# Weights of a two-layer attention decoder: splitting them in front of the pipeline, or as steps of its filling

## The chip, the cores and the metric

The kernel runs on one core of a Trainium2 chip. The metric is the device time of one execution in microseconds (us). Engines: TensorE (PE), VectorE (DVE), ScalarE (ACT), GpSimd (POOL); SyncE (SP) issues most DMAs.

## What is computed

64 batch elements, each with x (256 tokens x 256 channels) and a context (77 x 256), all float32, pass through two layers:

```
# layer 0, 16 heads of 64
x = x + softmax((rms(x)*norm_w @ wq) @ (ctx @ wk).T) @ (ctx @ wv) @ wo
# layer 1, 16 heads of 16; ln has a gain and a shift
x = x + causal_mha(ln1(x), ln1(x)) @ m_proj_w + m_proj_b
x = x + mha(ln2(x), ctx)           @ c_proj_w + c_proj_b
x = x + relu(ln3(x) @ f_w1 + f_b1) @ f_w2 + f_b2
```

## The kernel before

**Precision.** PE multiplies in an fp32r format. A float32 operand that needs more is held as a high half (`wh`, a rounding copy by ACT) and a low half (`wl`, value minus high half, by DVE), and a product is three matmuls (lines 1102 to 1104). For the weights this is done once, together with two foldings: the gain of the norm ahead of a product is multiplied into the weight, and the norm's shift times the weight is added to the bias.

**Three parts.** The main work is a list of steps in three orders, one for each engine, written out by hand: `HEAD` fills the pipeline (batches 0 and 1), `LOOP` is one turn and runs NB - 3 = 61 times, `TAIL` empties it. A word such as `qs0.0.1@1:6` is a step (scores of layer 0, tile 0, group 1), its batch and the PSUM bank it takes. PE, ACT and DVE each follow their own order. `full[s]` and `free[s]` are the semaphores of bank s: PE raises the first when a bank is filled, the reader raises the second. SP and POOL walk PE's order and do what hangs on some of its steps. The steps named below:

- `ctx`, `turn.0`: PE transposes the context and the normalised x; ACT copies the high half, DVE makes the low half. `rms`, `stat`, `norm`: statistics and normalisation.
- `q0`, `k0`, `v0`, `ck`, `cv`, `q1`, `k1`, `v1`: projections. `k0` and `ck` read weights that are not split (`wk0`, `wck`).
- `qs0`: scores of layer 0. DVE takes maxima (`/0`), ACT exponentials and sums (line 717), DVE divides (`/1`). `tr0` transposes them, `pv0` multiplies by `v0`, `wo` projects.
- `qsA`, `qsB`, `ln`, `mt`, `skA`, `skB`, `pv.1`: causal attention of layer 1.

The loop's order starts with `pv.1.1` (line 1299), so the first matmul of that line behind HEAD marks the loop's start.

**The setup.** All this begins when the weights are ready. Ahead of it runs a serial block, once for each of the twelve entries of `WEIGHTS` (line 509; f1 first, then f2, mq, mk, mv, cq, cv, mp, cp, wv0, wq0, wo0). f1, f2, wv0, wq0 and wo0 have 1 MB each, the others 256 KB. Entry i uses staging buffer i % 3. SP loads it (line 590) when DVE has released the buffer (`w_free`) and PE has drained (`w_bias`, line 1074). ACT makes the high half (lines 814, 816), DVE the low half (line 847). PE multiplies the staged weight by the shift, in columns of one (line 1062; f1, mq, mk, mv, cq) or, for the three row biases (f2, mp, cp), by a bias spread over 128 columns (line 1071), and DVE adds the product (lines 855, 873). DVE also spreads biases (lines 861, 866) and makes small tables (lines 876, 879). wo0 and f2 share one pair of tiles, `tail_h` and `tail_l`; their halves are stored to DRAM (`store_parts`, lines 580 and 581) and loaded again by POOL in every turn. Behind the twelve weights SP issues the first x and context (lines 595, 596), `wk0` and `wck`. DVE then raises `consts_ready`, for which ACT and PE wait before their first step:

```python
            act.wait_ge(consts_ready, 1)
            nc.scalar.preload_act_table_set("natural_log_exp_and_others")
            orders(act, run)
```

## Time and profile before

| | before |
|---|---|
| three runs | 5188.43 us median (5183.74 to 5189.82) |
| the profiled execution | 5188.64 us |
| its span | 5186.8 us |
| busy in the span | PE 5008.5 us (97%), ACT 4150.4 (80%), DVE 3032.0 (58%), POOL 698.2 (13%) |
| mean granted clock of PE | 0.988 |

The profile shows one execution. Its span runs from the first to the last instruction; the execution's own time is 1.8 us longer. Times in the rows below count from the span's start. PEclk is TensorE's granted clock as a share of 2.4 GHz. "idle before" is the time that the engine stood still ahead of an instruction, and the arrow names what ended it.

### The profile page before, as it was taken

Reading aid. Unit: us, or ns where it says so; the run is one execution under the profiler, and the core shown is the slowest. Engines: PE = TensorE matmul, PEld = TensorE weight load, DVE = VectorE, ACT = ScalarE, POOL = GpSimd, SP = SyncE. Lnnn points to the kernel's source line nnn. Section 1 sums busy time; section 2 is a strip of 40 time slices with the busy share of each in tenths; the row PEclk is TensorE's granted clock in tenths of the full one; section 3 lists DMA queues with packets and bytes.
Section 4 is the critical chain, followed back from the end, with each engine's and each line's share of the span. In section 5 each row is a group of like instructions: output and inputs, shape, how many; then the busy total and the mean of one; then the engine's idle time right before and its main releaser. Section 6 shows DMA issues by size and latency. Waiting matters only on the chain.

```text
span 5186.8 us, 148622 instructions
## 1 busy us (share of the span) xinstructions
PE 5008.5 (97%) x49240; PEld 4129.3 (80%) x49240; DVE 3032.0 (58%) x7921; ACT 4150.4 (80%) x17044; POOL 698.2 (13%) x1227
## 2 busy tenths in 40 slices
PE   7999999999999999999999999999999999999997
PEld 5788888888888888788888888888888888888875
DVE  4556655655655665665556556556656655565553
ACT  5788888888888888888888888888887888888874
POOL 0111111111111111111111111111111111111110
PEclk7999999999999999999999999999999999999997
DMA  3212112112112112121121121121121221211211
GB/s 111 74 45 76 62 56 79 62 56 78 62 56 78 49 70 78 42 76 67 53 76 62 56 79 62 56 78 57 62 78 44 74 76 44 76 62 56 79 58 37
DMA packets 101414, 337.76 MB, mean 65 GB/s; under 512 B 8720, under 2 KB 66896, under 8 KB 68048
## 3 DMA queue, kind: packets, MB, share of 16 engines
q0 software_dynamic: 36576, 266.35, 14.0%
q1 hardware_dynamic: 64496, 68.39, 4.0%
q14 instruction: 316, 2.59, 0.2%
q8 instruction: 26, 0.43, 0.0%
HBM read 313.74 MB, written 20.97 MB: 65 GB/s over the span
## 4 chain that ended last, share of the span: by engine, by line
PE 51%; ACT 30%; issue 10%; DVE 8%; DVEq 0%; DMA 0%; ACTq 0%; PEldq 0%; POOL 0%; SPq 0%; PEld 0%; POOLq 0%
ACT ps L717 23%; PE ps L1102 7%; PE ps L1104 6%; PE ps L1103 6%; PE ps L1282 5%; PE ps L1190 4%; PE ps L1299 4%; PE ps L1271 3%; DVE negmax L930 3%; PE ps L1260 3%; PE ps L1233 2%; PE ps L1248 2%; PE ps L1266 2%; ACT k0bd L697 2%; PE ps L1214 2%
## 5 line engine op out<-in xcount | busy, mean ns | idle before, releaser
L717 ACT ACTIVATE ps<-ps,negmax 128x77 f32<-128x77 f32 (+2 forms) x6144 | 2058.1, 366 | 308.2 <-DVE negmax L930 306.5
L717 ACT ACTIVATION_READ_ACCUMULATOR ps<-ps,negmax 128x1 f32 x6144 | 1455.7, 243 | 0.7
L930 DVE TENSOR_REDUCE negmax<-ps 128x4 f32<-128x308 f32 (+2 forms) x1792 | 923.6, 563 | 224.0 <-PE ps L1200 93.0
L651 POOL TENSOR_TENSOR small<-small 128x1 f32<-128x1 f32 (+1 forms) x448 | 257.9, 576 | 2556.8 <-DVE small L907 2300.7
L1102 PE MATMUL ps<-tail_h,coTh 128*128 128x256 f32 x2048 | 594.7, 290 | 3.9 <-DVE coTl L1030 3.4
L925 DVE TENSOR_TENSOR zTl<-ps,zTh 128x256 fp32r<-128x256 f32 x512 | 210.8, 422 | 628.0 <-ACT zTh L697 627.8
L1103 PE MATMUL ps<-tail_l,coTh 128*128 128x256 f32 x2048 | 574.2, 280 | 0.0
L1104 PE MATMUL ps<-tail_h,coTl 128*128 128x256 f32 x2048 | 572.9, 280 | 0.0
L789 ACT ACTIVATE probs<-ps 128x512 f32<-128x512 f32 x768 | 398.8, 616 | 130.3 <-PE ps L1271 130.3
L1102 PEld LDWEIGHTS ps<-tail_h,coTh 128*128 128x128 f32 x2048 | 386.5, 189 | 43.1 <-issue 34.6
L1103 PEld LDWEIGHTS ps<-tail_l,coTh 128*128 128x128 f32 x2048 | 387.4, 189 | 0.0
L1104 PEld LDWEIGHTS ps<-tail_h,coTl 128*128 128x128 f32 x2048 | 387.0, 189 | 0.0
L697 ACT COPY probs<-ps 77x512 f32<-77x512 f32 x512 | 285.7, 588 | 87.0 <-PE ps L1233 86.5
L1190 PE MATMUL ps<-k0bd,q0T 128*128 128x154 f32 x2048 | 351.1, 301 | 1.2 <-ACT ps L717 0.7
L697 ACT CAST zTh<-ps 128x256 fp32r<-128x256 f32 x512 | 192.9, 389 | 183.1 <-PE ps L1306 152.5
L1190 PEld LDWEIGHTS ps<-k0bd,q0T 128*128 128x128 f32 x2048 | 288.2, 191 | 31.3 <-issue 21.2
L786 ACT ACTIVATE probs<-ps 77x512 f32<-77x512 f32 x512 | 255.2, 602 | 70.4 <-PE ps L1248 70.4
L1102 PE MATMUL ps<-zTh,hi_f 128*128 128x256 f32 x1024 | 303.9, 297 | 5.8 <-issue 1.9
L1102 PE MATMUL ps<-xTh,hi_wq 128*128 128x256 f32 x1024 | 293.5, 287 | 0.3 <-ACT ps L717 0.3
L1103 PE MATMUL ps<-xTl,hi_wq 128*128 128x256 f32 x1024 | 286.4, 280 | 0.0
L1104 PE MATMUL ps<-xTh,lo_wq 128*128 128x256 f32 x1024 | 286.2, 279 | 0.0
L1103 PE MATMUL ps<-zTl,hi_f 128*128 128x256 f32 x1024 | 286.1, 279 | 0.0
(207 smaller groups left out, 12303.4 us busy)
## 6 DMA issues: line engine op xcount, KB each, us to landing
tail_h<-parted_f POOLq DMA_DIRECT2D x64, 1024.0 KB, 5.1
tail_l<-parted_f POOLq DMA_DIRECT2D x64, 1024.0 KB, 7.0
tail_h<-parted_wo POOLq DMA_DIRECT2D x63, 1024.0 KB, 5.2
tail_l<-parted_wo POOLq DMA_DIRECT2D x63, 1024.0 KB, 7.1
xin<-x_dram SPq DMA_DIRECT2D x64, 256.0 KB, 3.4
x<-x_dram SPq DMA_DIRECT2D x64, 256.0 KB, 2.7
out<-xr SPq DMA_DIRECT2D x64, 256.0 KB, 2.2
cin<-ctx_dram SPq DMA_DIRECT2D x64, 77.0 KB
```

The lines of the kernel that those rows point to most:

```text
L651: nc.gpsimd.tensor_tensor(rstd[:, stage, ts], veps[:, stage, ts], minus_half[:, ts], ALU.pow).then_inc(rstd_ready[stage], 1)
L697: return nc.scalar.copy(o, i)
L717: ins = nc.scalar.activation(scores, scores, ACT.Exp, bias=negmax[w][:, t, h:h + 1], accum_out=sums[w][:, t, h:h + 1])
L786: nc.scalar.activation(probs_slot(step, r)[0:S], bank(s)[0:S, :], ACT.Exp).then_inc(free[s], 1)
L789: nc.scalar.activation(probs_slot(step, r), bank(s), ACT.Exp).then_inc(free[s], 1)
L925: nc.vector.tensor_tensor(lo, src, hi, ALU.subtract).then_inc(free[s], 1)
L930: nc.vector.tensor_reduce(dst, bank(s)[:, 0:heads * width].rearrange("p (h k) -> p h k", h=heads), AX_X, ALU.max, negate=True).then_inc(ma ...
L1102: pe.matmul(o, lh, rh, start=first, stop=False)
L1103: pe.matmul(o, lh, rl, start=False, stop=False)
L1104: return pe.matmul(o, ll, rh, start=False, stop=last)
L1190: ins = pe.matmul(bank(s)[:, j * 2 * S:(j + 1) * 2 * S], q0T[:, m, t * P:(t + 1) * P], k0bd[:, m, :, :], start=True, stop=True)
L1282: ins = pe.matmul(bank(s)[D0 * e:D0 * e + D0, j * T:(j + 1) * T], v0[0:S, D0 * h:D0 * h + D0], probs_slot(("tr0", 0, i), e)[0:S, j * T:(j ...
```

## The change

The serial block is gone. What it did becomes three kinds of steps in HEAD's orders: `w.i` (split weight i: ACT's high half, DVE's low half), `b.i` (the product of weight i with a shift or a spread bias on PE, added by DVE; it takes a PSUM bank as any step) and `g.0` (the small tables, on DVE). `WEIGHTS` has a new order, and each entry its own staging place, in tiles that HEAD does not use yet (f1 and f2 in `probs1`, wv0 in `probs0`, wq0 in `q0T`, mq and mk in `k1bd`, cv in `z1`, mp in `x1`, ...); only wo0, cq and cp are loaded into a place that another had before. The gains, shifts and biases go from `probs0` to `logs`. PE waits for a weight (`have`) at the step of batch 0 that reads it. SP issues the first x and context, the small tables, and nine weights without a wait. The rest of HEAD's three orders and its banks are new too; LOOP and TAIL are as they were.

```diff
 HEAD_ORDER_TEXT = """
+ctx@0:0 rms@0 turn.0@0:1 k0.0@0:2 k0.1@0:3 q0.2@0:4 q0.1@0:5 q0.3@0:6 qs0.0.1@0:7 qs0.1.1@0:0 q0.0@0:1 rms@1
+v0.0@0:2 b.2@0:4 b.6@0:3 qs0.0.0@0:5 qs0.1.0@0:6 tr0.1.1@0:1 tr0.0.1@0:0 qs0.0.3@0:2 b.3@0:7 tr0.1.0@0:4 b.4@0:1
+b.5@0:0 b.8@0:6 tr0.0.0@0:7 qs0.0.2@0:3 b.9@0:5 qs0.1.2@0:4 pv0.1@0:2 tr0.0.3@0:3 qs0.1.3@0:4 pv0.0@0:7
+tr0.1.2@0:3 tr0.0.2@0:6 v0.1@0:6 tr0.1.3@0:3 pv0.2@0:4 pv0.3@0:6 ck@0:1 cv@0:0 ctx@1:5 b.10@0:3 wo.0@0:6
+stat.1.0@0 wo.1@0:4 k0.1@1:1 k0.0@1:2 stat.1.1@0 norm.1.0@0 norm.1.1@0 turn.1.1@0:0 turn.1.0@0:7 turn.0@1:5
+k1@0:3 q1.1@0:6 q0.1@1:4 qsB.0@0:1072 qsA@0:5364 q0.0@1:1 v1@0:0 qs0.0.1@1:7 q0.3@1:6 qs0.1.1@1:5 q0.2@1:2
...
 HEAD_ACT_ORDER_TEXT = """
+ctx@0 w.0@0 turn.0@0 k0.0@0 w.1@0 q0.2@0 k0.1@0 q0.1@0 w.2@0 q0.3@0 w.3@0 q0.0@0 qs0.1.1@0 qs0.0.1@0 v0.0@0 w.4@0
+w.5@0 w.6@0 w.8@0 w.7@0 tr0.1.1@0 qs0.1.0@0 tr0.0.1@0 qs0.0.0@0 qs0.0.3@0 tr0.1.0@0 w.11@0 w.9@0 qs0.0.2@0
+qs0.1.2@0 w.10@0 tr0.0.0@0 pv0.1@0 tr0.0.3@0 qs0.1.3@0 tr0.0.2@0 tr0.1.2@0 pv0.0@0 v0.1@0 tr0.1.3@0 pv0.2@0
+pv0.3@0 ck@0 ctx@1 cv@0 k0.1@1 turn.1.1@0 turn.1.0@0 k0.0@1 turn.0@1 k1@0 q1.1@0 q0.1@1 qsB.0@0/0 qsB.0@0/1
...
 HEAD_DVE_ORDER_TEXT = """
+rms@0 ctx@0 norm.0@0 w.0@0 turn.0@0 w.1@0 rms@1 w.2@0 qs0.0.1@0/0 qs0.1.1@0/0 w.3@0 qs0.1.1@0/1 qs0.0.1@0/1 b.2@0
+qs0.1.0@0/0 qs0.0.0@0/0 qs0.0.3@0/0 w.8@0 qs0.1.0@0/1 b.3@0 b.6@0 qs0.0.0@0/1 qs0.0.3@0/1 w.4@0 w.5@0 qs0.0.2@0/0
+w.7@0 qs0.1.2@0/0 w.9@0 qs0.0.2@0/1 qs0.1.2@0/1 w.10@0 qs0.1.3@0/0 b.8@0 w.11@0 qs0.1.3@0/1 w.6@0 b.4@0 b.5@0
+b.9@0 g.0@0 pv0.3@0 pv0.2@0 pv0.1@0 pv0.0@0 norm.0@1 ctx@1 b.10@0 wo.0@0 stat.1.0@0 norm.1.0@0 wo.1@0 stat.1.1@0
...
+        WEIGHTS = [("wq0", 0, None, flat(q0T)), ("wv0", None, None, flat(probs0)), ("f1", 3, 2, half[0]),
+                   ("f2", None, None, half[1]), ("mq", 1, 0, pair[0]), ("mk", 1, 0, pair[1]), ("mv", 1, 0, flat(q1T)),
+                   ("cv", None, None, flat(z1)), ("mp", None, None, flat(x1)), ("cq", 2, 1, half[1][:, 0:512]),
+                   ("cp", None, None, half[1][:, 512:1024]), ("wo0", None, None, half[0])]
...
@@ SP
+            sp.dma_start(xin[:], x_v[0]).then_inc(x_in, 16)
+            sp.dma_start(cin[0:S, :], ctx[0]).then_inc(c_in, 16)
+            for tile, n in small:
+                sp.dma_start(tile, w[n]).then_inc(consts_in, 16)
+            sp.dma_start(bias_h[:], w["f1b"]).then_inc(consts_in, 16)
+            for i in range(NUMBER["cq"]):
+                load(i)
+                if i < 2:
+                    tile, n = ((wk0, "wk0"), (wck, "ck"))[i]
+                    sp.dma_start(tile[:], w[n].rearrange("(k p) n -> p k n", p=P)).then_inc(plain_in[i], 16)
+            sp.dma_start(row[:, :, :], w["rows"].unsqueeze(0).to_broadcast([P, 3, C])).then_inc(rows_in, 16)
+
+            sp.wait_ge(x_used, 1)
+            sp.dma_start(xin[:], x_v[1]).then_inc(x_in, 16)
+            sp.wait_ge(c_used, 1)
+            sp.dma_start(cin[0:S, :], ctx[1]).then_inc(c_in, 16)
+
+            sp.wait_ge(w_lo, LO_COUNT[NUMBER["f1"]])
+            sp.wait_ge(hidden_spread, 1)
+            load(NUMBER["wo0"])
+            store_parts("f2")
+            sp.wait_ge(rows_made, ROW_COUNT["f2"])
+            load(NUMBER["cq"])
+            load(NUMBER["cp"])
+            sp.wait_ge(w_lo, LO_COUNT[NUMBER["mp"]])
+            sp.wait_ge(rows_made, ROW_COUNT["mp"])
             sp.dma_start(x1[:], x_v[0]).then_inc(xres_in, 16)
             store_parts("wo0")
@@ POOL
-                        if isinstance(b, int):
-                            pool.wait_ge(parts_out, 64)
...
+                if part.settle:
+
+                    pool.wait_ge(parts_out, 64)
@@ ACT
+                    elif n == "w":
+
+                        i = step[1]
+                        name, g, _, _ = WEIGHTS[i]
+                        act.wait_ge(w_in[i], 16)
+                        if name == "wo0":
+                            act.wait_ge(parts_out, 32)
...
+                        if isinstance(b, int) and b == 0:
+                            act.wait_ge(tables_made, 1)
...
-            act.wait_ge(consts_ready, 1)
+            act.wait_ge(consts_made, 9)
             nc.scalar.preload_act_table_set("natural_log_exp_and_others")
@@ DVE
+            def split_low(i):
+
+                n, g, _, _ = WEIGHTS[i]
                 src = staged(i)
+                dve.wait_ge(w_hi, HI_COUNT[i])
...
+            def add_product(u, i):
+
+                n, _, shifted, _ = WEIGHTS[i]
+                (s, v, _), = u["bank"]
+                dve.wait_ge(full[s], v)
...
+                if n == "f1":
+                    for k in range(MF):
+                        done(nc.vector.tensor_copy(hidden_rows(k), bias_h[:, k:k + 1].to_broadcast([P, P])))
+                    done(nc.vector.tensor_scalar(minus_bias[:], bias_h[:], -1.0, None, ALU.mult))
+                    dve.sem_inc(hidden_spread, 1)
@@ PE
-            for _ in range(30):
-                pe.wait_ge(consts_in, 16 * 4)
-            pe.wait_ge(consts_ready, 1)
-            pe.wait_ge(plain_in, 32)
+            for _ in range(26):
+                pe.wait_ge(consts_made, 9)
...
+            NEEDED = {"q0": "wq0", "v0": "wv0", "cv": "cv", "wo": "wo0", "tr0": "wv0"}
+
+            def have(n):
+
+                pe.wait_ge(w_lo, len(WEIGHTS) if n == "wo0" else LO_COUNT[NUMBER[n]])
+
+            def bias_product(u, i):
+                s = take_bank(u)
+                n, _, shifted, _ = WEIGHTS[i]
+                src = staged(i)
+                pe.wait_ge(w_in[i], 16)
...
+                    pe.wait_ge(hidden_spread if n == "f2" else value_spread, 1)
...
+                    if isinstance(b, int) and b == 0 and n in NEEDED:
+                        have(NEEDED[n])
+                    if n == "b":
+                        bias_product(u, step[1])
```

## Rows read from the trace of the kernel before

**Rows 1.** Windows: from:to, length, busy PE, PEld, DVE, ACT, POOL, PEclk, DMA, GB/s

```profile
0.00:55.40 55.40, 23.23 (x88) 19.74 (x88) 25.56 (x54) 17.91 (x20) 3.51 (x13) 0.74 0.66 229
...
64.51:92.28 27.77, 26.09 (x194) 22.36 (x194) 14.28 (x39) 22.42 (x92) 0.70 (x1) 0.95 0.01 2
92.28:147.01 54.73, 45.27 (x364) 33.72 (x364) 19.46 (x49) 34.44 (x138) 3.43 (x6) 0.81 0.02 7
...
147.01:225.67 78.66, 77.31 (x768) 64.29 (x768) 45.25 (x116) 64.57 (x266) 10.04 (x17) 1.00 0.18 63
...
304.53:4955.63 4651.10, 4563.56 (x45322) 3769.47 (x45321) 2772.01 (x7258) 3808.49 (x15695) 641.31 (x1122) 1.00 0.18 65
4955.63:5186.80 231.17, 187.61 (x1705) 147.99 (x1704) 106.52 (x276) 136.32 (x564) 27.64 (x48) 0.87 0.15 53
```

**Rows 2.** Waits in the setup: who waited for whom: us, times, longest

```profile
SPq L589 <- PEq L1074: 30.4, 9, 10.3
...
ACT hi_mv L816 <- DMA probs<-mv_dram: 7.9, 1, 7.9
```

**Rows 3.** Timeline of SP's DMA issues: start us, us, instruction

```profile
0.75 0.39 SPq L583 DMA_DIRECT2D bias_h<-f1b_dram  x1
...
2.62 0.95 SPq L590 DMA_DIRECT2D probs<-f_dram  x2
...
41.98 0.58 SPq L595 DMA_DIRECT2D xin<-x_dram  x1
```

**Rows 4.** Timeline of PE's matmuls: start us, us, instruction, idle before it

```profile
21.43 2.51 PE L1071 MATMUL ps<-probs,xr 128*128 128x256 f32 x8
...
24.21 1.02 PE L1062 MATMUL ps<-probs,q0T 128*128 128x1 f32 x8 [0.27 <-issue]
...
56.90 3.69 PE L1173 MATMUL ps<-cT,wk 128*128 128x77 f32 x16 [0.96 <-DVE cTl L925]
...
90.47 2.01 PE L1173 MATMUL ps<-cT,wk 128*128 128x77 f32 x16
```

**Rows 5.** Timeline of the setup: start us, us, instruction, idle before it

```profile
8.05 1.28 ACT L816 ACT_TABLE_LOAD   x1 [8.05 <-DMA probs<-f_dram]
...
8.12 6.96 PE L1062 MATMUL ps<-probs 128*128 128x1 f32 x32 [8.12 <-DMA probs<-f_dram]
9.35 2.19 ACT L816 ACTIVATE hi_f<-probs 128x1024 fp32r<-128x1024 f32 x2
...
11.64 2.48 DVE L847 SCALAR_TENSOR_TENSOR lo_f<-probs,hi_f 128x1024 fp32r<-128x1024 f32 x2 [6.08 <-ACT hi_f L816]
...
15.42 1.01 DVE L866 COPY xs<-bias_h 128x128 f32<-128x128 f32 x4
...
17.85 2.29 DVE L847 SCALAR_TENSOR_TENSOR tail_l<-probs,tail_h 128x2048 fp32r<-128x2048 f32 x1 [0.16 <-DVE minus_bias L867]
```

**Rows 6.** Windows, columns as in rows 1

```profile
5.00:10.00 5.00, 1.88 (x9) 1.91 (x10) 0.52 (x2) 1.93 (x2) 0.00 (x0) 1.00 1.05 384
...
66.00:67.00 1.00, 1.00 (x6) 1.00 (x6) 0.41 (x4) 0.00 (x0) 0.44 (x1) 0.50 0.00 0
```

**Rows 7.** Groups by line on DVE, 64.44 to 92.48 us: busy us, mean ns

```profile
L930 DVE TENSOR_REDUCE negmax<-ps 128x4 f32<-128x308 f32 x8 | 3.8, 476 | 5.5 <-PE ps L1190 5.3
L925 DVE TENSOR_TENSOR coTl<-ps,coTh 128x512 fp32r<-128x512 f32 x4 | 2.7, 686 | 3.9 <-ACT coTh L697 3.9
...
L972 DVE RECIPROCAL over<-sums 128x4 f32<-128x4 f32 x8 | 1.4, 176 | 2.7 <-ACT ps L717 2.5
```

**Rows 8.** Windows, columns as in rows 1

```profile
118.50:135.70 17.20, 14.29 (x90) 8.91 (x93) 7.54 (x20) 13.53 (x67) 0.00 (x0) 0.51 0.00 1
```

**Rows 9.** Chain that ended last, at the loop's entry: start us, us

```profile
145.96 1.05 issue
```

**Rows 10.** Timeline of PE at the first turn's jump

```profile
225.47 0.28 PE L1104 MATMUL ps<-tail_h,coTl 128*128 128x256 f32 x1
225.67 0.42 PE L1299 MATMUL ps<-probs,v 128*32 128x256 f32 x4
```

More of the change, by code:

```diff
@@ L100 @@
+b.9@0 g.0@0 pv0.3@0 pv0.2@0 pv0.1@0 pv0.0@0 norm.0@1 ctx@1 b.10@0 wo.0@0 stat.1.0@0 norm.1.0@0 wo.1@0 stat.1.1@0
+norm.1.1@0 turn.1.1@0 turn.1.0@0 turn.0@1 qsB.0@0/0 qsB.0@0/1 qsB.0@0/2 qsA@0/2 qsB.0@0/3 qsA@0/0 qsA@0/1 qsA@0/3
+qs0.0.1@1/0 qs0.1.1@1/0 qs0.0.1@1/1 qsB.1@0/0 qsB.1@0/2 qsB.1@0/3 qs0.0.0@1/0 qsB.1@0/1 qs0.0.3@1/0 qs0.1.0@1/0
+ln.1@0 qs0.1.0@1/1 qs0.1.1@1/1 qs0.0.0@1/1 qs0.0.3@1/1 pv.1.0@0
 """
@@ L604, in run @@
                     more = not isinstance(b, int) or b + 1 < NB
-                    if step == ("turn", 0) and more:
+                    first = isinstance(b, int) and b == 0
+                    if step == ("turn", 0) and more and not first:
                         sp.wait_ge(x_used, b + 1)
                         sp.dma_start(xin[:], x_at(x_v, b + 1)).then_inc(x_in, 16)
-                    elif n == "ctx" and more:
+                    elif n == "ctx" and more and not first:
                         sp.wait_ge(c_used, b + 1)
@@ L789, in run @@
                         nc.scalar.activation(probs_slot(step, r), bank(s), ACT.Exp).then_inc(free[s], 1)
+                    elif n == "w":
[5 more added lines that the diff above has]
+                        src = staged(i)
+                        for k in pieces(i):
+                            if g is None:
+                                ins = nc.scalar.copy(wh[name][:, k, :], src[:, k, :])
+                            else:
+                                ins = nc.scalar.activation(wh[name][:, k, :], src[:, k, :], ACT.Copy,
+                                                           scale=gain[:, g, k.start:k.stop])
+                        ins.then_inc(w_hi, 1)
                     elif n == "q1":
                         s = landed(u)
+                        if isinstance(b, int) and b == 0:
+                            act.wait_ge(tables_made, 1)
                         for m in range(KT):
@@ L806, in _ @@
             act.wait_ge(consts_in, 16 * 4)
-            for i, (n, g, s) in enumerate(WEIGHTS):
-                act.wait_ge(w_in[i % 3], 16 * (i // 3 + 1))
-                if n == "wo0":
-                    act.wait_ge(parts_out, 32)
-                src = staged(i)
-                for k in pieces(i):
-                    if g is None:
-                        nc.scalar.copy(wh[n][:, k, :], src[:, k, :]).then_inc(w_hi, 1)
-                    else:
-                        nc.scalar.activation(wh[n][:, k, :], src[:, k, :], ACT.Copy,
-                                             scale=gain[:, g, k.start:k.stop]).then_inc(w_hi, 1)
-            act.wait_ge(consts_ready, 1)
+            act.wait_ge(consts_made, 9)
             nc.scalar.preload_act_table_set("natural_log_exp_and_others")
@@ L1050, in _ @@
         def _(pe):
[L1051 to L1080 removed]
             for bank_full in full:
                 pe.sem_inc(bank_full, FIRST)
+            pe.wait_ge(consts_made, 9)
+            for _ in range(26):
+                pe.wait_ge(consts_made, 9)
             def take_bank(u, j=0):
@@ L1098, in landed @@
                         pe.wait_ge(free[s], v)
+            NEEDED = {"q0": "wq0", "v0": "wv0", "cv": "cv", "wo": "wo0", "tr0": "wv0"}
[4 more added lines that the diff above has]
+                n, _, shifted, _ = WEIGHTS[i]
+                src = staged(i)
+                pe.wait_ge(w_in[i], 16)
+                if shifted is not None:
+                    pe.wait_ge(consts_in, 16 * 4)
+                    for m in range(src.shape[2] // P):
+                        for k in range(KT):
+                            ins = pe.matmul(bank(s)[:, m:m + 1], src[:, k, m * P:(m + 1) * P], shift[:, shifted, k:k + 1],
+                                            start=(k == 0), stop=(k == KT - 1))
+                else:
+                    e = ("mp", "cp", "f2").index(n)
+                    pe.wait_ge(hidden_spread if n == "f2" else value_spread, 1)
+                    for k in range(src.shape[1]):
+                        rows = hidden_rows(k) if n == "f2" else z[:, e, k * P:(k + 1) * P]
+                        ins = pe.matmul(bank(s)[:, 0:C], rows, src[:, k, :], start=(k == 0), stop=(k == src.shape[1] - 1))
+                ins.then_inc(full[s], 1)
             def three(o, lh, ll, rh, rl, first, last):
@@ L1166, in run @@
                     elif n in ("k0", "ck"):
+                        if isinstance(b, int) and b == 0:
+                            pe.wait_ge(plain_in[0 if n == "k0" else 1], 16)
                         landed(c, u, step)
```

184 lines of the change are left out of this document (72 added, 112 removed).

## The prediction

> **What bounds the kernel now.** I read the windows first, cut at landmarks, because the change touches only what lies ahead of the loop. Four stretches of the span can be told apart [rows 1]. Up to 55.40 us the setup runs: TensorE (PE) is busy 23.2 us of it, VectorE (DVE) 25.6, ScalarE (ACT) 17.9, so three engines are each less than half full, one after another. Then comes the filling (HEAD) up to 147.01 us, when the first matmul of the loop's order starts. Then come 61 turns: (4955.63 - 147.01) / 61 = 78.83 us each, with PE busy 98% at a granted clock of 1.00. The last 231.17 us are the TAIL, which the diff leaves alone. The loop is 93% of the span and its text is not changed either. So the whole question is where the 147.01 us end, and whether a turn keeps its 78.83 us.
>
> Inside the setup the view of waits says why it is so loose [rows 2]: SP sat for 30.4 us in nine waits for PE's drain, because each of the three staging buffers is loaded again only when PE, ACT and DVE have left it; ACT then waits for the transfers behind it, once for 7.9 us. The first batch's x is issued only at 41.98 us, behind all weights [rows 3]. The reader is to see a chain load, split, drain, load, and no engine that is full.
>
> **The change, part by part.** I work out three stages: A, up to the first q0 product (before: 64.51 us); B, up to the first wo product (before: 92.28 us, 27.77 long); C, up to the loop (before: 147.01 us, 54.73 long) [rows 1, 4].
>
> *Stage A.* Twelve staging places replace three, so the loads are issued back to back: x, ctx, four small tables, then wq0 as the seventh. An issue costs SP 0.39 to 0.58 us [rows 3], so after six of them from 0.75 us on wq0 is issued at about 3.5 us. The first weight of the kernel before went out at 2.62 and PE could start on it at 8.12 [rows 3, 5]: 5.5 us. So wq0 lands at 9.0. It is cast on ACT (2.19 us, the row of f1, same size) up to 11.2 and subtracted on DVE (2.48 us) up to 13.7 [rows 5]. wk0 lies behind it on the same queue: 1.05 MB at 384 GB/s [rows 6] is 2.7 us, and with some slack for what shares the queue I set 11.9. The steps of ctx and of x's statistics need only x, ctx, GpSimd's identity and ACT's table load, all there by about 6 us, and are hidden behind wk0. PE then runs k0.0 and k0.1. Before, the first k0 matmul stood at 56.90, k0.0 took 3.69 us [rows 4], and q0 began at 64.51, 7.6 us later with x's turn in between; without it I take 7.4. The first q0 product starts at 11.9 + 7.4 = 19.3 instead of 64.51: 45.2 us earlier. Bounds: 17.5 (wk0 close behind wq0, no wait between) and 21.3 (both large transfers slowed as f1 and f2 were beside mq and the rows).
>
> Which clock do those products get? The granted clock reads 1.00 from the first microsecond, yet 32 matmuls of one column took 6.96 us at 8.12 (0.22 each) and eight of the same shape 1.02 us at 24.21 (0.13 each) [rows 4 to 6]. The durations decide: PE, idle up to 8 us, worked at its lower level of 1.2 GHz then and at 2.4 GHz later, and I take k0 at the lower one, as before at a granted clock of 0.50. The Trainium skill (TensorE: Matmul & The Clock Gate, Part 1: The HAM clock gate) says that the throttled clock is the default and that activity releases it; the durations agree with it and the column does not. By the column k0.0 and k0.1 would cost 2.01 us each, as the k0 at 90.47 does [rows 4], and stage A would end 3 us earlier.
>
> *Stage B* takes over most of what was setup. PE: its own busy time is 26.09 us; turn.0 and k0.0 of batch 1 leave for stage C (0.60 and 2.01), which leaves 23.5. The products come in. At the fast rate eight of the 128x1 matmuls take 1.02 us [rows 4]; f1 is 32 and mq, mk, mv, cq are 8 each, so eight such groups are 8.2. f2 is 16 of the 128x256 ones at 2.51 us per eight [rows 4], mp and cp are 4 each: 24 / 8 x 2.51 = 7.5. Sum 15.7, PE 39.2 us. At the rate of the setup it is 23.2 instead of 15.7 [rows 1]. DVE: 14.28 + 25.56, less 2.48 (w.0, stage A), 1.3 (x's statistics) and 0.69 (turn.0 of batch 1) = 35.4. ACT: 22.42 + 17.91, less 2.56 (two table loads), 2.19 (w.0) and 1.4 (k0.0 and turn.0 of batch 1) = 34.2. So three engines come out near 34 to 39 us: the stretch is no longer one engine's, and each wait between them shows.
>
> Walking the three orders with these durations: v0.0 ends on PE at 29; f1's product at 33; DVE has then done w.1, w.2, w.3, adds the product and makes eight spread copies (1.01 us for four, [rows 5]) by 36. Behind that one mark three things queue. PE's f2 product (b.3, 5.0 us) runs 37 to 42. SP issues wo0 and the two stores of f2's halves, 3.1 MB: at 384 GB/s 8.2 us plus some 2 us to land, so 46; ACT meets w.11, which waits for these stores, at 43 and stands for 3 us, and behind w.11 wait w.9, qs0.0.2 and all that follows on ACT. cq and cp are issued behind f2's product at 43 and land at 47, so b.9 waits there too. DVE after 36 still has six maxima (0.48), six divisions (a reciprocal of 0.18 and a multiply over the same 308 columns, taken as 0.48), eight low halves (2.29 for the 1 MB one, the others by their size, 7.9 in all), the other product adds with mv's four spreads (2.5), the small tables (2.4) and four context splits (0.69): 22.3 us of work and, by this walk, 5 us of waits, up to 63.3 [rows 5, 7]. wo.0 needs the last of them. Stage B is 63.3 - 19.3 = 44.0 us. Bounds: 39.2, PE's sum with no wait; and 52, PE at the slow rate (46.7) and 5 us of waits on top.
>
> *Stage C* has nothing of the setup but keeps its own work, and gets k0.0 and turn.0 of batch 1, 2.6 us. k0 goes into the hole between wo.1 and the turns, where q0.1 was, which moves behind q1.1. I add 1.6 us, between nothing and 2.6: 56.3. Of this stage 17.20 us ran at a granted clock of 0.51, beginning after a stretch where ACT's exponentials held PE up [rows 1, 8]. The new order has the same softmax blocks there, so I keep it. If it stayed at 1.00 up to 5 us would go, if the slow stretch grew by as much 4 would come: 50 to 60.
>
> What else is moved costs nothing on this path. The cp product (b.10), 4 matmuls in front of wo.0, is counted above. The x1 load comes behind the mp product near 47 and lands 16 us before DVE reads it. ACT's q1, k1 and ck wait for the small tables (61), as ck does by the walk for about 1 us, but only stage C reads kcbd. GpSimd's wait for the stores moves from wo.1 to the end of HEAD; they land long before, and no loop instruction gains a wait.
>
> **Sum.** The loop starts at 19.3 + 44.0 + 56.3 = 119.6 us instead of 147.01: 27.4 us earlier. The profiled execution took 5188.64 us (span 5186.8, 1.8 around it), the median of the runs is 5188.43, so I take the difference from the median: 5161.0.
>
> **Rivals.**
> 1. *The setup vanishes wholly.* Stages at their lower bounds: 17.5 + 39.2 + 50 = 106.7, that is 5148. For it: PE's idle time in B and C together is 11 us [rows 1]. Against: ACT is full for long in B and the chain through w.11. Chance 0.12.
> 2. *The engines take turns.* At the upper bounds 21.3 + 52 + 60 = 133.3, that is 5175; with PE slow in all of B and C's slow stretch too, some 5180, about no change. For it: the slow clock as late as 67 us, and again in C [rows 6, 8]. Against: PE has work without a break from 12 us on. Chance 0.10 beyond my range, a third of it within 0.2% of no change.
> 3. *A turn gets longer (the other side).* All engines' code ahead of the loop changes length, and a turn starts with a jump back. The price is that of one stall on the path a turn: at the entry to the loop the chain has 1.05 us of issue [rows 9]. 61 x 1.05 = 64 us, less 27: 5225. It decides from 27.4 / 61 = 0.45 us a turn (0.6 to be slower by over 0.2%). Against: at the jump of the first turn PE goes from its last matmul at 225.47 to the next at 225.67, with no stall to be seen [rows 10]; and the first turn, which was entered without a jump, is no shorter than the rest by more than 0.2 us [rows 1]. The Trainium skill (Runtime: NRT & Kernel Launch, Instruction fetch mechanics) says that a jump to code that is not held forces a fetch and a stall; by that rule where the loop begins in the code matters, and before, PE shows no such stall. Chance 0.06.
> 4. *It does not do what it says:* a step placed early on ACT or DVE waits for a late transfer and holds up all behind it, as if the setup were still serial. w.11 would have to be late by 17 more us to bring the gain to 10. Chance 0.04.
>
> **How the numbers follow.** My forecast has 0.68, with 5151 to 5172 as its own range. Rivals 1 and 2 lie at 5148 and 5175 to 5180. A range of 5149 to 5174 leaves out about a fifth: the outer halves of 1 and 2, and 3 and 4. Within 0.2% is within 10.4 us, about what a measurement of this kernel can tell from no change. Faster by more: all of the forecast and rival 1, most of 2: 0.88. Within: 0.06. Slower by more: 0.06, rival 3.
>
> **What would show it.** In the changed kernel's windows: the first k0 matmul near 12 us, q0 near 19; wo near 63; the first matmul of L1299's counterpart near 120; 61 turns of 78.8 us; a tail of 231 us. On the view of waits: ACT waiting for the stores before the last weight's cast for a few us, PE waiting for DVE before wo.0. The prediction is wrong if a turn differs by 0.2 us or more, if PE is held at 1.2 GHz in most of B, or if stage B is closer to 28 or to 55 us than to 44.

## The result, and the profile after

The changed kernel takes 5143.93 us (median of 4 runs, 5142.09 to 5148.35) against 5188.89 us of the kernel before on the same chip: a ratio of 0.9914 (95% interval 0.9901 to 0.9926), 45.0 us less. The forecast was 27.4 us less, with a range that ended at 5149. The direction is right and the size is not: the gain is 1.6 times what was forecast, and the largest extra part comes from where no gain was expected.

The profiled execution after took 5148.35 us (span 5146.4), 40.3 us less than the one before. Executions of one kernel lie up to some 10 us apart, and where they were profiled this goes with when PE's clock falls to its lower level in the filling: the profiled one of the changed kernel is the slowest of its four, 4.4 us above their median, and those of before_counts and before_dve_one (below) enter the loop at 153.97 and 152.95 us, where the kernel before does at 147.01. The windows of the changed kernel, cut at the same landmarks as [rows 1]: the first q0 product, the first wo product, the first matmul of the loop's order (now line 1361), the end of the first turn, the start of the tail.

```profile
0.00:18.06 18.06, 8.42 (x38) 7.85 (x39) 5.89 (x14) 6.95 (x8) 4.23 (x14) 1.00 0.84 300
18.06:69.21 51.15, 45.37 (x262) 37.75 (x262) 32.69 (x82) 32.40 (x106) 1.68 (x1) 0.80 0.48 169
69.21:123.23 54.02, 44.68 (x382) 35.21 (x383) 21.46 (x55) 34.83 (x139) 3.44 (x6) 0.86 0.02 6
123.23:203.96 80.73, 79.62 (x768) 65.05 (x768) 45.17 (x116) 64.70 (x266) 10.04 (x17) 0.96 0.17 61
203.96:4915.52 4711.56, 4636.21 (x46089) 3818.85 (x46088) 2813.04 (x7381) 3882.27 (x15961) 652.97 (x1141) 1.00 0.18 65
4915.52:5146.40 230.88, 187.49 (x1705) 147.87 (x1704) 106.77 (x276) 136.55 (x564) 27.65 (x48) 0.87 0.15 54
```

| stretch | before | forecast | after | after less forecast |
|---|---|---|---|---|
| A, to q0 | 64.51 | 19.3 | 18.06 | -1.2 |
| B, to wo | 27.77 | 44.0 | 51.15 | +7.2 |
| C, to the loop | 54.73 | 56.3 | 54.02 | -2.3 |
| first turn | 78.66 | 78.7 | 80.73 | +2.1 |
| 60 turns, each | 78.83 | 78.83 | 78.53 | -0.30 (-18.4 in all) |
| tail | 231.17 | 231 | 230.88 | -0.3 |

Two things stand out: stage B is 7.2 us too long, and 60 turns whose text was not touched are 18.4 us shorter in all (4729.96 to 4711.56 us, 78.833 to 78.526 each). The landmarks themselves, on PE's timeline:

```profile
11.22 7.11 PE L1235 MATMUL ps<-cT,wk 128*128 128x77 f32 x32 [1.98 <-DMA wk<-wk_dram]
...
18.42 0.41 PE L1159 MATMUL ps<-xTl,hi_wq 128*128 128x256 f32 x1
...
19.83 0.28 PE L1160 MATMUL ps<-xTh,lo_wq 128*128 128x256 f32 x1
...
69.21 0.36 PE L1158 MATMUL ps<-tail_h,coTh 128*128 128x256 f32 x1 [0.56 <-issue]
...
123.23 1.93 PE L1361 MATMUL ps<-probs,v 128*32 128x256 f32 x16 [3.01 <-ACT probs L823]
```

*Stage B.* SP's timeline first. The issue of mq stood for 6.58 us, where the others take 0.4 to 1.4. 5.5 MB of weights (five of 1.05 MB, and wck) had been issued ahead of it, and none of them had landed when it began. So the second batch's x, the last but one of that block, went out at 17.87 us only.

```profile
5.83 1.00 SPq L600 DMA_DIRECT2D probs<-f_dram  x2
6.88 6.58 SPq L600 DMA_DIRECT2D k1bd<-mq_dram  x1
...
17.87 0.79 SPq L615 DMA_DIRECT2D xin<-x_dram  x1
...
36.42 0.37 SPq L600 DMA_DIRECT2D probs<-wo_dram  x1
36.84 0.58 SPq L596 DMA_DIRECT2D parted_f<-tail_h  x1
37.46 0.43 SPq L597 DMA_DIRECT2D parted_f<-tail_l  x1
```

DVE, which has `rms@1` ahead of `w.2`, stood until this x was there, and ACT's first exponentials behind it:

```profile
25.70 0.75 DVE L943 BATCH_NORM_STATS2 stats<-xin 128x6 f32<-128x256 f32 x2 [5.66 <-DMA xin<-x_dram]
...
27.15 2.48 DVE L898 SCALAR_TENSOR_TENSOR lo_f<-probs,logs,hi_f 128x1024 fp32r<-128x1024 f32 x2
```
```profile
30.43 0.30 ACT L751 ACTIVATE ps<-ps,negmax 128x77 f32<-128x77 f32 x1 [3.10 <-DVE negmax L979]
...
48.25 1.90 ACT L834 CAST tail_h<-probs 128x2048 fp32r<-128x2048 f32 x1 [6.29 <-DMA parted_f<-tail_l]
```

The last row is the wait that the forecast named, at `w.11` for the stores of f2's halves, but 6.3 us long instead of 3: ACT was there at 41.96 us instead of 43, and the last store landed 10.7 us after its issue, at 48.2 us instead of 46. From 36.42 to 48.20 us the DMA engines moved 297 GB/s, cq and cp included, where the forecast took 384. Behind the stores lay cq, which landed later still, 7.5 us after its issue at 41.44 us, so at 48.9. From the view of DMA issues (size, us from issue to landing):

```profile
parted_f<-tail_l SPq DMA_DIRECT2D x1, 1024.0 KB, 10.7
probs<-cq_dram SPq DMA_DIRECT2D x1, 256.0 KB, 7.5
```

Two steps wait for cq: `b.9` on PE, and `w.9`, the next in ACT's order behind `w.11`. PE's idle time is the one for cq; the arrow names no releaser, but the wait ended 0.1 us behind cq's landing, and so it did in after_x_early (below), where cq landed at 46.5 us:

```profile
48.98 1.02 PE L1146 MATMUL ps<-logs,probs 128*128 128x1 f32 x8 [3.89 <-issue]
```

The windows around it, columns as in rows 1:

```profile
45.00:50.00 5.00, 1.11 (x10) 1.05 (x10) 1.82 (x5) 1.75 (x1) 0.00 (x0) 1.00 0.74 290
50.00:62.50 12.50, 11.29 (x43) 6.80 (x43) 9.18 (x23) 8.22 (x34) 0.00 (x0) 0.52 0.31 116
```

PE was busy 1.1 of 5 us, and then worked for 12.5 us at a mean granted clock of 0.52, nearly throughout at its lower level of 1.2 GHz.

*The turn.* The wait values of a PSUM bank's semaphores are `turn * uses a turn + count at the loop's entry`, kept in registers. HEAD now uses the banks otherwise, so the counts at the entry are 35, 34, 34, 36, 36, 32, 38, 34 where they were 34, 34, 34, 36, 34, 33, 32, 34. The built program derives one value from another by an addition where it can, and with other counts these additions stand at other places: on PE 86 lone ones in the loop instead of 84, on ACT 84 instead of 82, on DVE 90 as before, but elsewhere. No line of LOOP was edited, and yet its instructions are not the same. Whether that makes the 0.3 us is what most experiments are about.

### The profile page after: what moved, and what is told of

Its sections match the earlier page's. It is cut to its first block, busy times and chain, and to the rows that moved or that the text cites. A ratio compares the mean times of both kernels' runs of the same rounds, so it can differ in the third digit from the quotient of the medians.

```text
span 5146.4 us, 148723 instructions
## 1 busy us (share of the span) xinstructions
PE 5001.8 (97%) x49240; PEld 4112.6 (80%) x49240; DVE 3025.0 (59%) x7921; ACT 4157.7 (81%) x17043; POOL 700.0 (14%) x1227
## 4 chain that ended last, share of the span: by engine, by line
PE 50%; ACT 30%; DVE 9%; issue 8%; DVEq 1%; ACTq 0%; POOL 0%; POOLq 0%
ACT ps L751 24%; PE ps L1158 7%; PE ps L1160 5%; PE ps L1159 5%; PE ps L1252 4%; PE ps L1295 4%; DVE negmax L979 4%; PE ps L1361 4%; PE ps L1333 3%; PE ps L1322 3%; PE ps L1344 3%; PE ps L1310 2%; PE ps L1328 2%; PE ps L1166 2%; PE ps L1276 1%
## 5 line engine op out<-in xcount | busy, mean ns | idle before, releaser
L1160 PE MATMUL ps<-zTh,lo_f 128*128 128x256 f32 x1024 | 287.7, 281 | 0.0
```

Of the source, the lines that this page charges most:

```text
L1160: return pe.matmul(o, ll, rh, start=False, stop=last)
```

## The experiments

All times are medians, the ratio is to the kernel before on the same chip (5188.9 to 5192.0 us on those used, so compare ratios and not times across rows), and a turn is the mean of the 60 distances between 61 y stores of the profiled execution (by which the kernel before has 78.817 us and the changed one 78.510). "idle" is read in a steady turn: DVE's aggregator (BATCH_NORM_AGGREGATE) ahead of the spread context, the step from the instruction behind it to the start of the context's copy `cT`, and what ACT stands for behind both.

| kernel | us | ratio, 95% interval | turn | aggregator idle | step to cT | ACT idle |
|---|---|---|---|---|---|---|
| before | | 1 | 78.817 | 0.26 | 0.29 | 0.74 |
| changed | 5143.93 | 0.9914, 0.9901 to 0.9926 | 78.510 | 0.17 | 0.20 | 0.48 |
| before_counts | 5174.79 | 0.9966, 0.9954 to 0.9978 | 78.542 | 0.26 | 0.20 | 0.58 |
| after_counts | 5162.01 | 0.9939, 0.9925 to 0.9953 | 78.695 | 0.17 | 0.29 | 0.65 |
| after_equal | 5147.97 | 0.9912, 0.9899 to 0.9926 | 78.477 | 0.26 | 0.20 | 0.58 |
| after_shifted | 5149.23 | 0.9915, 0.9900 to 0.9930 | 78.537 | 0.16 | 0.20 | 0.48 |
| before_bank6 | 5163.11 | 0.9947, 0.9933 to 0.9960 | 78.408 | 0.17 | 0.20 | 0.48 |
| before_banks045 | 5186.52 | 0.9997, 0.9988 to 1.0006 | 78.803 | 0.16 | 0.30 | 0.65 |
| before_shifted | 5177.99 | 0.9977, 0.9968 to 0.9986 | 78.647 | 0.16 | 0.29 | 0.64 |
| before_dve_one | 5182.76 | 0.9988, 0.9979 to 0.9997 | 78.723 | 0.16 | 0.29 | 0.65 |
| after_store | 5138.40 | 0.9896, 0.9881 to 0.9911 | 78.447 | 0.17 | 0.20 | 0.49 |
| after_x_early | 5141.79 | 0.9900, 0.9885 to 0.9915 | 78.497 | 0.17 | 0.20 | 0.48 |
| after_both | 5140.01 | 0.9899, 0.9883 to 0.9914 | 78.447 | 0.17 | 0.20 | 0.49 |
| after_best | 5131.19 | 0.9884, 0.9869 to 0.9899 | 78.377 | 0.16 | 0.20 | 0.48 |

### The counts at the loop's entry

Only the number at which both sides of a bank begin to count is changed, and with it the registers' values and the additions in the loop:

```diff
-FIRST = 24
+FIRST = [25, 24, 24, 24, 26, 23, 30, 24]    # before_counts
+FIRST = [23, 24, 24, 24, 22, 25, 18, 24]    # after_counts
+FIRST = [23, 24, 28, 24, 22, 28, 24, 24]    # after_equal
```

**before_counts**, the kernel before with the loop's instructions of the changed one:

> The kernel before, whose eight bank semaphores start at other values (25, 24, 24, 24, 26, 23, 30, 24 instead of 24 each), so that they stand at the loop's entry as in the changed kernel; setup, orders and banks are those of before. The instructions of a turn are then, register additions and waits, those of the changed kernel. Theory 'counts' (the turn is shorter by 0.31 us because the wait values and with them the register additions of the loop changed): the turn falls from 78.83 to 78.53 us, the loop starts at 147.0 us as before, the total is 5189 - 61 x 0.31 = 5170. Rival 'position' (the code of the loop stands at another place behind another setup): the turn stays 78.8, the total 5189. Rival 'entry' (the pipeline enters the loop in another phase and keeps it): 5189 as well.

**after_counts**, the changed kernel with the loop's instructions of the kernel before:

> The changed kernel, whose bank semaphores start at 23, 24, 24, 24, 22, 25, 18, 24, so that they stand at the loop's entry as in the kernel before. Theory 'counts': the turn goes back up to 78.83 us and the total to 5144 + 19 = 5163, 26 below the kernel before, which is then what the overlapped setup alone brings. Rivals 'position' and 'entry': the turn stays 78.53 and the total 5144.

**after_equal**, the changed kernel with fewer additions in the loop:

> The changed kernel with starts 23, 24, 28, 24, 22, 28, 24, 24: banks 2 and 6, which are taken 15 times a turn, and banks 3 and 5, taken 14 times, then share their wait values, and a turn has fewer register additions (79 instead of 86 on PE, 80 instead of 84 on ACT, 89 instead of 90 on DVE). Theory 'counts', if it is the number of additions in front of waits that costs: the turn is at or below 78.53 us, perhaps 78.3, the total 5130 to 5144. If it matters only where an addition stands, the turn can be anywhere from 78.3 to 78.8. Rivals 'position' and 'entry': 78.53.

before_counts gave 5174.79 us, 16.9 less than the kernel before on that chip (5191.68), and a turn of 78.542 us with the old setup in front: 61 times the 0.275 us are 16.8, so most of the 0.3 us go with the counts and not with the setup. after_counts gave 5162.01 us, and its turn goes back by 0.185 us, but only to 78.695 us, 0.12 short of the kernel before with the same loop instructions. It keeps 0.61% of gain, 24 to 39 us by the interval. By its profile 24.0 us of that lie ahead of the loop, which starts at 122.98 us, and 7.3 in the 60 turns. after_equal has twelve additions fewer in the loop than the changed kernel and no measurable difference, so their number does not decide it. Where they stand does, as one place on DVE shows. after_counts, a steady turn:

```profile
2055.99 0.18 DVE L947 BATCH_NORM_AGGREGATE mv<-stats 128x2 f32<-128x6 f32 x1 [0.16 <-DVE stats L943]
2056.20 0.15 DVE L956 TENSOR_SCALAR small<-mv 128x1 f32<-128x1 f32 x1
2056.49 0.32 DVE L1014 COPY cT<-ps 128x154 f32<-128x154 f32 x1
```

and the changed kernel at the same place:

```profile
2054.40 0.18 DVE L947 BATCH_NORM_AGGREGATE mv<-stats 128x2 f32<-128x6 f32 x1 [0.17 <-DVE stats L943]
2054.61 0.15 DVE L956 TENSOR_SCALAR small<-mv 128x1 f32<-128x1 f32 x1
2054.81 0.32 DVE L1014 COPY cT<-ps 128x154 f32<-128x154 f32 x1
```

From `small` to `cT` it is 0.29 us where two additions (for the count of line 1011 and that of line 1013) stand between, 0.20 us where one does: 0.09 us for one addition. DVE is what ACT waits for here: it stands for the maxima behind it, 0.65 us in the one and 0.48 us in the other. after_counts, then the changed kernel:

```profile
2057.67 0.45 ACT L751 ACTIVATE ps<-ps,negmax 128x256 f32<-128x256 f32 x1 [0.65 <-DVE negmax L979]
```
```profile
2055.99 0.45 ACT L751 ACTIVATE ps<-ps,negmax 128x256 f32<-128x256 f32 x1 [0.48 <-DVE negmax L979]
```

PE shows a difference of the same size: it idles 0.26 us for ACT ahead of the products of line 1344, and 0.17 us with the new counts (after_counts, then the changed kernel). Which addition makes it was not taken apart.

```profile
2027.99 1.95 PE L1344 MATMUL ps<-probs,v 77*64 77x256 f32 x16 [0.26 <-ACT probs L731]
```
```profile
2026.43 1.95 PE L1344 MATMUL ps<-probs,v 77*64 77x256 f32 x16 [0.17 <-ACT probs L731]
```

### One bank, and the other three

**before_bank6** has `FIRST = [24, 24, 24, 24, 24, 24, 30, 24]`, **before_banks045** `[25, 24, 24, 24, 26, 23, 24, 24]`.

> The kernel before with the count of one bank, the seventh, begun at 30 instead of 24 for both sides, as the changed kernel's head leaves it; nothing else. The other three banks whose counts differ stay as before, the head and the tail run the same instructions. Theory (the 0.3 us a turn come from where the additions for the waits' values fall, and most of the loop instructions that moved, on PE around the products and on DVE and ACT ahead of the spread context, are those of this bank): a turn of 78.55 to 78.65 us, total 5172 to 5178. Rival (another bank's count carries it, or only the sum of all four): 78.78 to 78.83 us a turn and 5186 to 5190.

> The kernel before with the counts of the other three banks that the changed kernel leaves differently (first 25, fifth 26, sixth 23 instead of 24), the seventh as before. Theory (the seventh bank's 6 carry the gain of a turn, and the other three took some of it back: with it alone 78.41 us, with all four 78.54, before 78.82): a turn of 78.82 to 78.95 us, total 5188 to 5200. Rival (the shares don't add, each set of counts gives a placement of its own): anything between 78.4 and 78.8, total 5165 to 5188.

The seventh bank alone gives 78.408 us a turn and 5163.11 us, a larger gain than all four together (78.542) and below the range that was expected; the other three give 78.803 us and no measurable difference. So the shares of the banks do not add, and the changed kernel's counts, which nobody chose, are not the best. before_banks045 also shows how a gain is lost again: ACT stands 0.65 instead of 0.74 us for DVE's maxima, as in other faster versions, but in each steady turn PE then stands 0.43 instead of 0.36 us for DVE ahead of `mparts` (the kernel before, then before_banks045):

```profile
2068.45 0.41 PE L1225 MATMUL ps<-ident,mparts 128*128 128x128 f32 x2 [0.36 <-DVE mparts L989]
```
```profile
2067.28 0.41 PE L1225 MATMUL ps<-ident,mparts 128*128 128x128 f32 x2 [0.43 <-DVE mparts L989]
```

### The place of an instruction

What of the 0.12 us between the kernel before and after_counts, whose loops have the same instructions? **after_shifted** and **before_shifted** put idle instructions ahead of the loop, 8 on PE and 3 or 4 on ACT and DVE. From before_shifted (after_shifted repeats `consts_made` waits instead, 42 instead of 26 on PE):

```diff
-            dve.wait_ge(consts_in, 16 * 4)
+            for _ in range(8):
+                dve.wait_ge(consts_in, 16 * 4)
...
-            for _ in range(30):
+            for _ in range(46):
                 pe.wait_ge(consts_in, 16 * 4)
```

> The changed kernel with more waits that are met at once ahead of HEAD (8 instructions more on PE, 3 on ACT, 4 on DVE), so that the loop's code stands elsewhere on these engines while nothing in a turn changes. Rival 'position': the turn moves by some 0.1 us or more, the total by 6 us or more. Theory 'counts' and rival 'entry': the turn stays 78.53, the total 5144 within 3.

> The kernel before with idle waits ahead of the loop, so that its loop stands 8 instructions later on PE and 3 later on ACT and DVE; the loop's own instructions are the same. It is meant for the 0.12 us a turn by which the changed kernel with the old counts (78.70) is shorter than the kernel before (78.82), with the same loop instructions. If the place in the code does it: a turn at least 0.05 us off 78.82, total 3 us or more from the kernel before's. If not: 78.80 to 78.84 us, total within 2 us.

after_shifted left the turn (78.537) and the ratio (0.9915) where they were; its 5149.23 us lie above the expected 5144 within 3, on a chip where the kernel before is 2.8 us slower too. The theory of the place seemed to fall, and before_shifted brought it back: 0.170 us less a turn (78.647) and 10.9 us in all. Its DVE shows where 0.1 us of it is. The copy `cT` comes as late behind `small` as before, but the aggregator ahead of it idles 0.16 us. before_shifted, then the kernel before:

```profile
2079.64 0.18 DVE L900 BATCH_NORM_AGGREGATE mv<-stats 128x2 f32<-128x6 f32 x1 [0.16 <-DVE stats L896]
2079.86 0.15 DVE L909 TENSOR_SCALAR small<-mv 128x1 f32<-128x1 f32 x1
2080.15 0.32 DVE L961 COPY cT<-ps 128x154 f32<-128x154 f32 x1
```
```profile
2083.35 0.18 DVE L898 BATCH_NORM_AGGREGATE mv<-stats 128x2 f32<-128x6 f32 x1 [0.26 <-DVE stats L894]
2083.56 0.15 DVE L907 TENSOR_SCALAR small<-mv 128x1 f32<-128x1 f32 x1
2083.86 0.32 DVE L959 COPY cT<-ps 128x154 f32<-128x154 f32 x1
```

In all the traces read for it this idle time goes with one number, the aggregator's index in DVE's program: 0.26 us where it is 321 (before, before_counts, after_equal), 0.16 to 0.17 us at 320, 322, 323, 324 and 326. **before_dve_one** tests that with one idle instruction more on DVE, and nothing else:

```diff
-            dve.wait_ge(consts_in, 16 * 4)
+            for _ in range(3):
+                dve.wait_ge(consts_in, 16 * 4)
```

> The kernel before with one idle instruction more ahead of the loop, on DVE alone; PE, ACT and all instructions of the loop are where and what they were. In eleven traces DVE's aggregator ahead of the spread context idles 0.26 us where it is instruction 321 of DVE's program (before, before_counts, after_equal) and 0.16 to 0.17 us where it is 320, 322, 324 or 326. Theory (the place of this one instruction costs 0.1 us a turn, and that is the 0.12 us between the changed kernel with the old counts and the kernel before): the aggregator idles 0.16 us, ACT's wait for the maxima behind it 0.64 to 0.66 instead of 0.74 us, a turn of 78.65 to 78.74 us, total 5178 to 5184. Rival (PE's or ACT's place did it in the shifted kernel, or the moment at which the loop is entered): the aggregator stays at 0.26 us or the turn at 78.80 us or more, total 5187 to 5190.

It came out as expected by the theory: the aggregator at index 322 idles 0.16 us, ACT 0.65 us, the turn is 78.723 us (0.094 less) and the total 6.2 us less, with an interval (0.9979 to 0.9997) that just leaves out no difference. The edit moves all of DVE's loop instructions by one; the aggregator's idle time is the one that changes most among them. before_shifted gained 0.076 us a turn more than this, with PE and ACT moved as well, which was not taken apart. Here is the aggregator in before_dve_one:

```profile
2089.36 0.18 DVE L899 BATCH_NORM_AGGREGATE mv<-stats 128x2 f32<-128x6 f32 x1 [0.16 <-DVE stats L895]
```

### Stage B

**after_store** lets SP store f2's halves when they are made, **after_x_early** issues the second x and context behind f2's load, **after_both** does both:

```diff
+            store_parts("f2")                        # after_store
-            sp.wait_ge(w_lo, LO_COUNT[NUMBER["f1"]])
             sp.wait_ge(hidden_spread, 1)
             load(NUMBER["wo0"])
-            store_parts("f2")
@@ for i in range(NUMBER["cq"]):
                 load(i)
+                if WEIGHTS[i][0] == "f2":            # after_x_early: the four lines
+                    sp.wait_ge(x_used, 1)            # stood behind the load of the rows
+                    sp.dma_start(xin[:], x_v[1]).then_inc(x_in, 16)
+                    sp.wait_ge(c_used, 1)
+                    sp.dma_start(cin[0:S, :], ctx[1]).then_inc(c_in, 16)
```

> The changed kernel with one edit: SP stores the two halves of f2 as soon as they are made, ahead of its wait for the spread copies and ahead of wo0's load. Theory (stage B holds a queue of ACT behind these stores): the stores land near 40 us, ACT's 1.9 us at the split of wo0 for the landing is gone, the steps behind it start up to 5 us earlier (ACT's copy at 43 instead of 48.25 us), PE is idle less between 45 and 50 us, the loop starts at 118 to 121 us instead of 123.23, total 5139 to 5142. Rival (wo0's load, 1 MB, now lands later by as much, or DVE is the bound there): the start of the loop within 1 us of 123.23 and the time within 2 us of the changed kernel's. The turn, whose code is not touched, stays 78.52 us within 0.03 in both.

> The changed kernel with one edit: the loads of the second batch's x and context are issued right behind f2's load, and not behind all weights and the rows. Theory (DVE stood at the second x's statistics until 25.7 us, and ACT's first exponentials behind that): x lands by 20 us, w.2's low half starts at 24.6 instead of 27.15 us, ACT's 3.1 us ahead of the first exponentials shrinks, the loop starts about 2.5 us earlier than 123.23, total about 5141.5. Rival (SP now waits for the first x to be used, up to 11 us, with mq, mk and the rest behind it, and the weights land later): no gain or a loss of up to 3 us at the loop's start. The turn stays 78.52 us in both.

> The two edits together (f2's stores ahead of wo0's load, and the second x issued behind f2). Theory: the two waits lie one behind the other on the same path, so the gains add: the loop starts 5 to 7.5 us earlier, total 5137 to 5139. Rival (PE at its lower clock and the queue of 3.1 MB set the stage's end, whatever stands in front): less than 2 us together, 5142 to 5144.

after_store: the stores go out at 32.53 us, ACT stands 1.19 us instead of 6.29, and `w.11` begins at 43.04 us. Stage B is 46.41 us, at a clock of 0.85; C is 51.13 at 0.96, where it was 54.02 at 0.86; the loop starts at 115.60. ACT's row, and the windows of B and C:

```profile
43.04 1.90 ACT L833 CAST tail_h<-probs 128x2048 fp32r<-128x2048 f32 x1 [1.19 <-DMA probs<-wo_dram]
```
```profile
18.06:64.47 46.41, 43.54 (x263) 36.60 (x262) 32.40 (x82) 32.48 (x106) 1.68 (x1) 0.85 0.52 187
64.47:115.60 51.13, 40.48 (x382) 32.40 (x383) 21.35 (x55) 34.62 (x139) 3.42 (x6) 0.96 0.02 7
```

The edit moves two landings. The stores no longer hold up `w.11`, and cq, no longer behind them, lands at 44.1 instead of 48.9 us:

```profile
probs<-cq_dram SPq DMA_DIRECT2D x1, 256.0 KB, 3.0
```

By ACT's order, with the first alone it would have stood again at `w.9`, for cq, until 48.9 us; that was not run by itself. So the 7.6 us at the loop's start are what a queue free of the stores is worth, and not the price of one wait. One part of what was expected missed: the turn, whose code on PE, ACT and DVE is untouched, was to stay at 78.52 us within 0.03 and is 78.447. after_both has the same 78.447 and after_x_early 78.497; the first two have one instruction less ahead of the loop on SP, the third has none less. That was not tested further. It means that a few hundredths of a microsecond a turn between two versions say nothing about their counts.

after_x_early: ACT's first exponentials come at 28.22 instead of 30.43 us, the loop starts at 120.41, 2.8 us earlier, as the theory said. But the two do not add. In after_both `w.11` begins at 41.70 us, earlier than in either, and the loop only at 120.00 us, 3.2 us earlier where 5 to 7.5 were expected: stage B is 48.8 us long, at a clock of 0.76.

```profile
18.06:66.87 48.81, 46.49 (x262) 39.22 (x262) 33.32 (x84) 32.81 (x106) 0.70 (x1) 0.76 0.50 176
```

PE is busy 46.49 us there and 43.54 us in after_store, for the same matmuls: the 3 us are the clock's, not a wait's. PE is at its lower level for 10.3 us in after_store and for 17.1 in after_both, from about 50 us on in both, though neither has the idle time for cq ahead of it:

```profile
49.80:60.10 10.30, 9.54 (x38) 5.67 (x39) 7.08 (x20) 4.65 (x15) 0.00 (x0) 0.50 0.59 229
```
```profile
50.30:67.40 17.10, 16.34 (x64) 11.24 (x64) 10.64 (x28) 7.55 (x23) 0.00 (x0) 0.50 0.37 143
```

What puts PE there was not tried. Nor is the difference one of the whole kernel. The first turn has a stretch at the lower level in after_store and none in after_both:

```profile
115.60:196.38 80.78, 79.70 (x768) 65.06 (x768) 45.09 (x116) 64.57 (x266) 10.02 (x17) 0.96 0.18 61
```
```profile
120.00:198.06 78.06, 76.98 (x769) 63.64 (x769) 45.11 (x116) 64.57 (x266) 10.03 (x17) 1.00 0.18 63
```

So 4.4 us between the two at the loop's start are 1.7 a turn later; the profiled executions took 5137.75 and 5137.80 us, and the medians, 5138.40 and 5140.01, lie within each other's runs (after_store 5137.75 to 5141.43, after_both 5137.80 to 5142.07). The second edit is worth nothing measurable on top of the first. Each of these stage times is read from one execution.

### The best version

**after_best** is after_store with `FIRST = [23, 24, 24, 24, 22, 25, 24, 24]`, which gives the changed kernel the loop of before_bank6:

> The changed kernel with f2's stores moved ahead of wo0's load, and the banks' counts begun so that the loop is entered with the counts of the kernel before, but the seventh bank's 6 higher (the seventh at 38), as in the kernel before with that bank's count alone. Theory (a turn's length goes with the counts at the loop's entry, whatever stands ahead of the loop): a turn of 78.30 to 78.42 us, 0.03 to 0.15 below the version with the stores alone, total 5130 to 5136. Rival (the 78.41 us hold only behind the old setup): 78.45 us or more, total 5138 or more.

5131.19 us, and a turn of 78.377: better than both kernels, 57.7 us less than the kernel before and, by the ratios, some 15 us less than the changed one (0.9884 to 0.9914, of 5189). The turn is 0.07 shorter than after_store's, about 4 us in 61. The loop starts at 116.49 us. Its filling is after_store's, and yet its stage B is 44.29 us against 46.41 and its C 54.14 against 51.13: so far can one execution's stages lie from another's.

## Why the prediction was right and wrong

**What was right.** Stage A: k0 came at 11.22 us (11.9 forecast) and q0 at 18.06 (19.3), wk0's landing was the last wait, and k0 ran at the lower clock, 7.11 us for both halves, though the column says 1.00. The Trainium skill (TensorE: Matmul & The Clock Gate, Part 1: The HAM clock gate) says that the throttled clock is where PE starts; durations of 0.41 us at 18.42 and 0.28 us at 19.83 us for matmuls of one shape agree, the column does not. The first entry of the clock in this trace stands at 19.7 us, just where the durations change, so the column's 1.00 ahead of it is no measurement. `w.11` waited for the stores, as the chain was put.

**What looks right and is not.** after_counts, the changed kernel with the turn's counts undone, took 5162.0 us against 5161.0 forecast. That is luck. Its filling gained 24.0 us where 27.4 were forecast, and its turn, 0.12 us shorter than the kernel before's, gave 7 more; and the kernel before takes 5191.7 us on that chip, so that by the ratio (0.9939) the time to set beside the forecast is 5157.2.

**The step that failed** is "The loop is 93% of the span and its text is not changed either", from which the turn's 78.83 us were carried over. Rival 3 took the turn up, but only as a jump's stall that makes it longer, with a threshold of 0.45 us a turn; a turn shorter by 0.3 us was in no case. The forecast's own sign of being wrong, a turn that differs by 0.2 us or more, came true. The text of the loop is the source's. What runs depends also on the counts with which the loop is entered and on the index of its instructions, and HEAD's new order changed both. The runs split the 0.307 us: 0.185 come with the counts (after_counts to the changed kernel), and 0.122 with what else differs ahead of the loop (before to after_counts). Of these 0.122, DVE's place by one instruction makes 0.094 (before_dve_one; DVE's loop stands one instruction later in after_counts too), with the aggregator off index 321; the other 0.028 are open, and no larger than what after_store shows without any such edit. The shares are not sums of local costs: from the other side the counts give 0.275 (before to before_counts), though the aggregator stays slow there, and before_banks045 has a fast aggregator and a turn only 0.014 us shorter, with 0.07 us more of PE's idle time ahead of `mparts`. What makes index 321 slow stays open. The Trainium skill (Runtime: NRT & Kernel Launch, Instruction fetch mechanics) says that a jump to code that is not held makes the engine fetch and stall. Rival 3 used that rule, and the traces bear out only that place matters: the cost seen sits in the middle of DVE's turn, not at its jump, and it is 0.1 us, a tenth of the 1.05 us by which the rival was priced.

**Stage B, 44.0 against 51.15 us**, names the right wait and is short in its sizes. ACT's stand at `w.11` was 6.3 instead of 3 us (11.8 us from wo0's issue to the last store's landing, where 8.2 + 2 were taken, without cq and cp on the same queue). That cq lands late was foreseen for `b.9` (47, measured 48.9), not for `w.9`, which stands behind `w.11` on ACT. Taking the stores out of the way gave 7.6 us at the loop's start, the clock's part included. The wait of `rms@1` for x was left out of the walk: SP's issues were costed at 0.4 to 0.6 us each, and one stood for 6.58; undoing it alone gave 2.8 us at the loop's start, and on top of the other edit nothing measurable. And PE's sum was taken at the fast rate (39.2), while 45.4 us were measured at a mean clock of 0.80. The bounds of 39.2 to 52 held.

**Stage C and the first turn** agree in their sum, 54.02 + 80.73 = 134.75 us against 56.3 + 78.7 = 135.0, but by luck. C had a mean clock of 0.86 instead of 0.81, and the long stretch of [rows 8] became several short ones, the last from 122.1 to 128.9 us, across the loop's entry:

```profile
122.10:128.90 6.80, 5.67 (x40) 3.36 (x41) 0.42 (x1) 0.70 (x3) 0.00 (x0) 0.50 0.01 2
```

In after_counts, whose filling has the same instructions, that last stretch is missing: its first turn took 78.29 us at a clock of 1.00, and with its C of 53.79 the sum is 132.1.

```profile
122.98:201.27 78.29, 77.05 (x768) 63.94 (x769) 45.21 (x116) 64.55 (x266) 10.05 (x17) 1.00 0.18 63
```

**The sum.** From the forecast in the profile's own times, 5188.64 - 27.4 = 5161.2: -1.2 + 7.2 - 2.3 + 2.1 - 18.4 - 0.3 = -12.9, that is 5148.3, and the profiled execution took 5148.35. The median is another 4.4 us lower, for which no trace was taken. Without the turn's part the profiled execution would have taken 5166.8 us and the median would be 5162.3, both inside the range. The turn alone carried the result out of it, and stage B's error, of the other sign, hid 7 us of that.

## What to carry to other kernels

A loop body is only the same if its built instructions are: where wait values are register sums, a change ahead of the loop moves additions within it, and one of 0.09 us is worth 5.5 us in 61 turns where nothing else takes it back, so compare the built loops before carrying a turn's time over. Vary the start counts and put an idle instruction ahead of the loop before giving a difference of a few tenths of a per cent to the edit that was made. When loads are issued back to back, put the one that is read first ahead of the bulk, and store results before asking for the next megabyte; then measure the two together, because here they did not add. And where one edit moves two landings on a queue, do not book its gain on the wait that you had in mind.
